# The ending of a fused transformer block without sixteen unread products

## The reference, cut to what matters

```python
x = x + xattn(_layernorm(x), ctx_1024, ctx_1024, mask, ...)   # attention over 257 keys of a context
x = x + retention(_layernorm(x), ...)                         # decayed scores, gate, output product
x = x + ffn(_layernorm(x), W1, b1, W2, b2)
# ffn: both products on 8-bit activations (per token) and ternary weights
def bitlinear(x, W, b):
    x_scale = clip(max(abs(x), axis=-1), EPS)
    xq = clip(round(x * (127 / x_scale)), -128, 127) * (x_scale / 127)
    return einsum('bnd,hd->bnh', xq, Wq) + b
h = gelu(bitlinear(x, W1, b1));  out = bitlinear(h, W2, b2)   # 512 -> 2048 -> 512
```

## Time and profile before

| | us |
|---|---|
| median of 3 runs | 741.67 |
| lowest and highest run | 741.49, 743.29 |
| the profiled execution | 741.27 |
| its span, first to last instruction | 739.48 |
| PE busy | 709.2 |
| DVE busy | 406.5 |
| ACT busy | 326.5 |
| POOL busy | 202.7 |

### The profile page before, as it was taken

How to read it: one execution, slowest core, us unless ns; L and a number is a source line. 1 busy time by engine, 2 the same in 40 slices (tenths; PEclk the granted TensorE clock), 3 DMA queues, 4 the chain that set the end, 5 groups by cost and what they waited for, 6 DMA issues and landing times.

```text
span 739.5 us, 18487 instructions
## 1 busy us (share of the span) xinstructions
PE 709.2 (96%) x7369; PEld 575.9 (78%) x7384; DVE 406.5 (55%) x1089; ACT 326.5 (44%) x700; POOL 202.7 (27%) x160
## 2 busy tenths in 40 slices
PE   4999999999999999999999999999998999999976
PEld 1788888888888888888888888877776767766743
DVE  4833323323665345345343323349478888887886
ACT  3425456455344344344344344455224524433434
POOL 2610001000987647647530000001122122113110
PEclk9999999999999999999999999999999999999999
DMA  7242333332132231231121121626001011101201
GB/s 256 93 175 61 120 122 107 128 121 89 36 122 84 89 118 35 89 117 36 32 64 32 32 64 33 228 60 242 1 1 30 1 42 43 43 1 43 43 1 44
DMA packets 46632, 56.83 MB, mean 77 GB/s; under 512 B 15088, under 2 KB 35824, under 8 KB 45328
## 3 DMA queue, kind: packets, MB, share of 16 engines
q1 hardware_dynamic: 41840, 39.20, 17.3%
q0 software_dynamic: 3328, 16.78, 6.4%
q10 hardware_dynamic: 1440, 0.53, 0.3%
HBM read 51.19 MB, written 2.16 MB: 72 GB/s over the span
## 4 chain that ended last, share of the span: by engine, by line
PE 82%; DVE 10%; issue 4%; DMA 2%; ACT 1%; SPq 0%; DVEq 0%; POOL 0%; ACTq 0%
PE bank L231 66%; PE bank L437 4%; PE bank L595 3%; PE bank L451 3%; PE bank L428 3%; DVE s_sb L1388 2%; DMA stage<-in_w_xq 2%; PE bank L558 1%; DMA stage<-in_w_xo 1%; DVE X L1446 1%; DVE y_quant L1354 1%; DVE h_max L1395 1%; DVE h_sb L1372 0%; DVE y_sb L1363 0%; PE bank L459 0%
## 5 line engine op out<-in xcount | busy, mean ns | idle before, releaser
L231 PE MATMUL bank<-ctx_high,wk_high 128*128 128x258 f32 x512 | 147.4, 288 | 0.1
L231 PE MATMUL bank<-ctx_low,wk_high 128*128 128x258 f32 x512 | 144.6, 282 | 0.0
L231 PE MATMUL bank<-ctx_high,wk_low 128*128 128x258 f32 x512 | 144.1, 282 | 0.0
L231 PEld LDWEIGHTS bank<-ctx_high,wk_high 128*128 128x128 f32 x512 | 96.8, 189 | 13.7 <-issue 13.4
L231 PE MATMUL bank<-wv_high,ctx_high 128*128 128x512 f32 x256 | 105.9, 414 | 0.0
L791 ACT ACTIVATE vals<-bank 128x512 f32<-128x512 f32 x64 | 38.3, 598 | 144.2 <-PE bank L231 144.2
L231 PE MATMUL bank<-wv_low,ctx_high 128*128 128x512 f32 x256 | 101.2, 395 | 0.0
L231 PE MATMUL bank<-wv_high,ctx_low 128*128 128x512 f32 x256 | 100.9, 394 | 0.0
L231 PEld LDWEIGHTS bank<-ctx_low,wk_high 128*128 128x128 f32 x512 | 96.7, 189 | 0.0
L231 PEld LDWEIGHTS bank<-ctx_high,wk_low 128*128 128x128 f32 x512 | 96.5, 188 | 0.0
L781 ACT ACTIVATE kT<-bank,bxk 128x257 f32<-128x257 f32 x128 | 60.3, 473 | 56.5 <-PE bank L231 56.3
(11 more groups left out here) (217 smaller groups left out, 1359.0 us busy)
## 6 DMA issues: line engine op xcount, KB each, us to landing
raw<-in_ctx_t SPq DMA_DIRECT2D x32, 514.0 KB, 4.0
stage<-in_w POOLq DMA_DIRECT2D x16, 1024.0 KB, 5.9
X<-in_x SPq DMA_DIRECT2D x4, 512.0 KB, 4.2
v_last<-last_values SPq DMA_DIRECT2D x32, 64.0 KB
out<-X SPq DMA_DIRECT2D x8, 256.0 KB, 2.3
stage<-in_w_xv SPq DMA_DIRECT2D x1, 1024.0 KB, 8.1
stage<-in_w_xq SPq DMA_DIRECT2D x1, 1024.0 KB, 11.5
stage<-in_w_xk SPq DMA_DIRECT2D x1, 1024.0 KB, 5.7
```

The source lines that it names most:

```text
L231: last = pe.matmul(to, left(i, c), right(j, c), start=(c == 0 and i + j == 0), stop=(c == C - 1 and i == 1))
```

## The change

The helper `keep_running` and its one call are taken out. The wait for `h_biased` that stood ahead of the call stays, and the next instruction of TensorE is the first turn of `turn_quantised(T - 1)`, which waits for `y_ready`. Nothing else differs.

```diff
-            def keep_running(count):
-
-                for _ in range(count):
-                    pe.matmul(bank[3][:, :], yqT[:, 0, :], w1q[:, 0, 0:512], start=True, stop=True)
-
...
             feed_down(T - 3, range(FC - 2, FC))
             pe.wait_ge(h_biased, 4 * (T - 1))
-            keep_running(16)
             turn_quantised(T - 1)
             turn_hidden_half(T - 2, 0)
             feed_up(T - 1, (0,))
```

## The result

The changed kernel took 743.67 us (median of 12 runs, 742.61 to 745.16) and the kernel before 741.92 us (12 runs beside them, 741.31 to 743.54): 1.75 us more between the medians. Over all the runs the ratio is 1.0022, with a 95% interval of 1.0014 to 1.0030. The forecast was 743.6, with a range of 742.4 to 745.3. The profiled execution took 742.92 us with a span of 741.1. The mean granted clock of a run, 0.999 in the profiled execution of before, is 0.998 or less in each of the twelve runs of the changed kernel and 0.993 in three of its four slowest.

The account below looks back on a forecast made before the run. VectorE sets the time until yq, then TensorE is on the path. Products' removal gains 0 and a clock fall costs 1.9 us: 741.67 + 1.9 = 743.6 us, range 742.4 to 745.3.

Parts of the forecast that it names:

- The products gain nothing by going: Sixteen products ahead of yq: removal frees some 3.5 us of TensorE, none on the path; gain 0.
- The clock falls: TensorE's wait ahead of yq, grown to 4.5 us: clock drops to 1.2 GHz between about 718 and 720.5.
- The clock comes back 4.3 us after the work: After the wait ahead of yq: clock rises 4.3 us after work resumes, at 724.8 or 725.7.
- The 1.9 us: Loss on TensorE's path from 721.37, taken as the middle of 1.7 and 2.15 us.
- Half of the low stretch on the path is lost: TensorE's turns and up products from 721.37: half of the half-speed time is lost, 1.7 to 2.15 us.
- It is carried whole to the end, and the down products stay hidden: Behind 725.89: the 1.9 us reaches the end whole; sixteen down products, 3.62 us, stay hidden before the rounded quarter.
- The rival of a second fall: Wait of 1.51 us at 729.34: clock falls again, 1.7 us more lost, 745.3 us; chance 0.15.
- The clock that stays down to the end: From TensorE's wait ahead of yq to the end: low clock costs about 11 us, 752.6 us; chance 0.02.
- The forecast's class: Whole kernel: 0.26% slower, inside the 0.3% that counts as the same; chance of within 0.3% was 0.62.

Follow-up runs that it names:

- fill_second_only: Changed kernel plus six unread products in TensorE's 1.51 us wait for the last tile's rounded quarter; median 744.12 us, ratio 1.0022 to the kernel before.
- fill_both: Kernel before, sixteen products kept, plus six unread products in TensorE's 1.51 us wait for the rounded quarter; median 741.89 us, ratio 0.9990.
- start_only: Kernel before, sixteen products kept, plus six identity products in TensorE's wait for query weights near 18 us; median 741.88 us, ratio 0.9988.
- eight_late: Kernel before with eight products in place of sixteen, held back until VectorE has centred the tile; median 742.00 us, ratio 0.9996.
- late_eight_filled: Kernel before with eight products released by y_scaled in place of sixteen, start's and rounded quarter's waits filled; median 742.04 us, ratio 0.9985.
- eight_early: Kernel before with eight products in place of sixteen, issued at once when TensorE is free; median 743.24 us, ratio 1.0013.
- first_wait_only: Changed kernel with the start's and rounded quarter's waits filled, only the wait ahead of yq left open; median 743.87 us, ratio 1.0013.

## Why the prediction was right, point by point

- **The products gain nothing by going.** Right. yq takes 0.43 us and comes 0.23 us later than before, which is the offset of the start. TensorE waited 4.46 us for it.
- **The clock falls.** Right in the fact, wrong in the moment: the forecast said 718 to 720.5, inside the wait. Measured were 720.99 in the changed kernel, just behind the wait, and 722.5 with eight early products; with the second wait filled it was 720.1, inside it. The 2.0 us between the last product and the fall in the earlier trace rows was read as a delay that holds everywhere; it is not one.
- **The clock comes back 4.3 us after the work.** The term was taken too firmly. It came back 3.6 us after the first turn in the changed kernel (724.40 - 720.84) and 5.1 us in fill_second_only. The 1.9 us built on it lie between the 1.36 us of the one profile and the (726.9 - 722.59) / 2 = 2.2 us of the other, 722.59 being where the turns of hq start there. By medians the term measured 1.75 us against before and 2.08 us with the other waits filled. The start of the program, from which the 4.3 us were read, gives over 5.8 us in fill_both and at most 3.7 in fill_second_only. The mechanism was right; that the median, 743.67, came within 0.1 us of the forecast is partly luck, since the two executions lose 1.36 and some 2.2 us and the forecast took a middle for another reason.
- **Half of the low stretch on the path is lost.** Right: 1.40 by the rule and 1.36 measured. The bf16 turns and products slow down as the f32 ones of the earlier trace rows do, the eight turns from 0.62 to 1.04 us.
- **It is carried whole to the end, and the down products stay hidden.** Right: the wait for the rounded quarter is 1.51 us in both.
- **The rival of a second fall** was described rightly (1.7 us forecast, 1.66 measured in start_only) and charged wrongly: it was counted for the changed kernel alone, from a trace in which it had not happened. The kernel before is open to it too: start_only, which shows it, differs from before at the start alone. A third fall, at the start, stands in the profiles of fill_second_only and eight_late, whose start is that of before. Such falls widen the runs of before and may cancel in part from the difference. How many of the changed kernel's runs have the second one is not shown; its profile does not, and filling that wait brought no gain (fill_second_only). That the one run of before at 743.29 us was such a fall fits its height; that run has no trace.
- **The clock that stays down to the end** is shown by no profile: behind the waits of the ending it was back after 3.4 or 6.8 us.
- **The forecast's class**, slower by 0.26% and inside the 0.3%, holds: 0.22%.

## What to carry to other kernels

A wait of the matrix engine costs more than its length when the clock falls behind it: look for what is on the path in the next few microseconds and count half of the low stretch. Work that nobody reads can pay for itself in a wait that another engine ends, if it ends before that; eight products late in the wait did as much as sixteen from its beginning, and eight at its beginning did not (742.00, 741.99 and 743.24 us). And one trace at full clock does not prove that the clock holds in every run: compare the spread of the runs, not only the profile.

## What the runs showed of the hardware that was not expected

- A wait of 1.51 us of TensorE brought the fall in one execution (start_only, 733.0) and not in another of the same place (the kernel before), with the same instructions around it. A wait of 1.98 us brought it in late_eight_filled (719.7) and not in eight_late.
- The fall is not tied to the moment at which TensorE stops: it came 2.0 us after the last product at the end of before and 4.6 us after it in the changed kernel, there 0.15 us after work had begun again.
- The low stretch behind a wait of the ending lasted 3.4 us in five of these profiles (changed kernel, eight_early, start_only, first_wait_only, late_eight_filled) and 6.8 us in fill_second_only.
